# Twenty-four key/value units spread otherwise over an attention kernel: six, not eight, ahead of the first head pair

## The chip, the cores and the metric

One core of a Trainium2 chip (trn2) runs the whole kernel in one launch. The metric is the device time of one execution in microseconds, lower is better. Before: a median of 2206.81 us over 3 runs (2203.21 to 2211.9).

## What is computed

`x` is 8 images of 768 channels by 32x32 places (1024 tokens), float32. Layer 0 is group norm, a token attention with 12 heads of 64, and a residual; layer 1 is group norm, a per-channel integer shift with a separable 3x3 filter, and a residual. The attention is unusual: query and key enter only by their variance over the 64 channels of a head, so each head's scores are the outer product of two vectors.

```
qkv = tokens(gn(x)) @ W_qkv.T ;  q, k, v per head of 64
scores = var(v) x var(k) * 64**-0.5          # 1024 x 1024, rank one
x = x + proj(softmax(scores) @ v) + b_proj
x = x + depthwise3x3(shift(gn(x), offset))
```

## The kernel before, in words

**One image** goes through four stages. *Phase C* of the image before (line 1182): the projection, 12 tiles of 128x512 outputs, each 18 matmuls. *Phase A* (1152): the first key/value units. A unit (1076) is 36 fp16 matmuls that make k and v of two blocks of 128 tokens for one pair of heads; 4 units (`UQ`) make a pair and 24 an image. *The span* (1162): 6 pairs `p` of heads, each with 8 steps `m` of 128 keys. At each step ScalarE makes two tiles of exponentials (`exps`, 583), VectorE adds them up for the denominator (`add_up`, 786; steps 1 to 6 of pairs 0 to 3, 1 to 4 of pairs 4 and 5), and TensorE weighs v with them (`weigh`, 1117); a pair ends with the denominators on TensorE (1108, called at 1180). The units of pairs 2 to 5 are put into the steps of pairs 0 to 3, two at m = 0 and two at m = 4. `run` (276) makes image 0 by itself, loops six times over the middle images and ends with the last two; all but image 0 also do layer 1 of the image before inside the span.

**What a unit leads to.** VectorE takes its statistics (`kv_stats`, 742), ScalarE copies v out (`v_evict`, 576). Unit u + 2 waits for both, since they share two PSUM banks. After a pair's fourth unit VectorE forms the variances (`variances`, 752), TensorE transposes them (`k_transpose`, 1098), VectorE takes the key maximum and copies the row `at` (`k_max`, 767), TensorE spreads the maximum (`k_spread`, 1104), and VectorE makes the coefficients (`k_scales`, 777) with which that pair's exponentials start. SyncE writes `at` to HBM (`a_write`, 383) and reads it back broadcast to 128 partitions (`a_broadcast`, 387), the input of `exps`.

**What a pair's end leads to.** ScalarE copies the denominators (`d_copy`, 600, at m = 3 of the next pair), SyncE moves them in four small DMAs (`d_rows`, 396), VectorE inverts them (`d_reciprocal`, 802, at m = 2 in its own order), SyncE writes and broadcasts them (`r_write`, 402, `r_broadcast`, 406), VectorE normalises (`o_normalise`, 806), ScalarE and VectorE split the result in two fp16 parts (`o_first`, 611, `o_second`, 813). After pair 5 nothing of the span is left beside this, and the projection of the last part waits for it.

**What sets the order.** Each engine runs its own list in order, written out by hand in `span` and `phase_a` of each engine (SyncE 416, ScalarE 623, VectorE 862, TensorE 1152); semaphore waits stand in the list, so a wait holds up all behind it. VectorE's span before is

```
add_up(m) ; m=2: d_reciprocal, kv_stats ; m=3: kv_stats, k_max, taps_y, gn
m=4: k_scales, o_normalise ; m=5: kv_stats ; m=6: kv_stats, variances, taps_x ; m=7: o_second
```

The next image's `x` is loaded over `h_sp` (the input of all units) from ScalarE's queue, once no unit reads it any more; its statistics go over HBM on SyncE's queue (`stats_to_groups`, 324) in `group_end` (923). In image 0, `beside_a` (1204) transposes the 12 pieces of the projection's weights beside phase A.

Of the kernel before, what the change touches and what calls it, by code (L numbers as in the profile page):

```python
# [38 lines left out]
def gn_attention_displace(nc, x, w_qkv, w_proj, b_proj, offset, out):  # L39
# [17 lines left out]
    PC = 4 * HD  # L57
    UQ = MT // 2
    NU = NP * UQ
    RING = 8  # L60
# [22 lines left out]
    with ctx:  # L83
# [239 lines left out]

        def stats_to_groups(sp, k, b):
            sp.wait_ge(s_stat[k], b + 1)
            sp.dma_start(cs_rows[k].rearrange("(t p) s -> p t s", p=P), mv[k][:, :, :]).then_inc(s_cs[k], 16)
            sp.wait_ge(s_cs[k], b * 16 + 16)
            sp.dma_start(gin[k][:, :, :], cs_rows[k].rearrange("(g c) s -> g c s", c=GC)).then_inc(s_gin[k], 16)

        def stats_out(sp, k, b):  # L330
# [51 lines left out]
        def _(sp):  # L382
# [33 lines left out]
            def span(b, l1, with_next):  # L416
                later = l1 is not None
                a_write(b, 0)
                a_broadcast(b, 0, later)
                for p in range(NP):  # L420
                    if p == 0:
                        a_write(b, 1)
                        a_broadcast(b, 1, later)
                        continue
                    d_rows(b, p - 1)
                    r_write(b, p - 1)
                    if p < NP - 1:
                        a_write(b, p + 1)
                    r_broadcast(b, p - 1, later)
                    if p < NP - 1:  # L430
                        a_broadcast(b, p + 1, later)
                d_rows(b, NP - 1)
                r_write(b, NP - 1)
                r_broadcast(b, NP - 1, later)
                if with_next:
                    stats_to_groups(sp, "x", b + 1)
                    stats_out(sp, "x", b + 1)
                    stats_to_channels(sp, "x", b + 1)
# [116 lines left out]
        def _(act):  # L555
# [4 lines left out]
            def make_h(b):  # L560
# [4 lines left out]
                for t in range(CT + 1):  # L565
# [3 lines left out]
                    if t:  # L569
                        h_first(b, t - 1)  # L570

            def load_x(b, tiles):
                for t in tiles:
                    act.dma_start(x_in[:, t, :], x_t[b, :, t, :]).then_inc(s_xin[t], 16)
# [48 lines left out]
            def phase_a(b, beside=None):  # L623
                for u in range(2 * UQ - 1):
                    v_evict(b, u)
                    if beside is not None:
                        beside(u)

            def span(b, l1, with_next, beside=None):
                later = l1 is not None  # L630
                for p in range(NP):
                    nxt = (p + 2) * UQ
                    for m in range(MT):
                        if not later and p == 0 and m == 3:
                            act.wait_ge(s_pads, 2 * CT * 16)
                        exps(b, p, m)
                        if m == 1 and p == 0:
                            v_evict(b, 2 * UQ - 1)
                        if m == 3:
                            if p:  # L640
                                d_copy(b, p - 1, later)
                            if later:
                                middle_tap(l1, p)
                            if p <= 3:
                                v_evict(b, nxt)
                                v_evict(b, nxt + 1)
                        if m == 7:
                            if p:
                                o_first(b, p - 1)
                            if 1 <= p <= 4:  # L650
                                add_bias(b, p - 1)
                            if p <= 3:
                                v_evict(b, nxt + 2)
                                v_evict(b, nxt + 3)
                        if with_next and (p, m) in ((4, 1), (4, 4), (4, 7)):
                            load_x(b + 1, (2 * (m // 3), 2 * (m // 3) + 1))
                        if beside is not None:
                            beside(p, m)
# [12 lines left out]
            def beside_a(u):  # L671

                if u == 2:
                    act.wait_ge(s_scale, 2)
                if u >= 2:
                    weight_first(WKU + 2 * (u - 2))
                    weight_first(WKU + 2 * (u - 2) + 1)

            def beside_span(p, m):

                if (p, m) == (0, 0):
                    for w in range(2 * (2 * UQ - 1 - 2), WU - WKU):
                        weight_first(WKU + w)
                if (p, m) == (1, 0):
                    act.wait_ge(s_sub, 1)
                    nc.scalar.activation(taps[:, :, :, :], taps[:, :, :, :], ACT.Exp, scale=-2.0).then_inc(s_tapexp, 1)
# [34 lines left out]
        def _(dve):  # L721
# [140 lines left out]
            def phase_a(b, l1, beside=None):  # L862
                for u in range(2 * UQ - 1):
                    kv_stats(b, u)
# [17 lines left out]
            def span(b, l1, with_next, beside=None):  # L882
                later = l1 is not None
                for p in range(NP):
                    nxt = (p + 2) * UQ
                    if p == 0:
                        kv_stats(b, 2 * UQ - 1)
                        variances(b, 1)
                    for m in range(MT):
                        add_up(b, p, m, later)  # L890
                        if m == 2:
                            if p:
                                d_reciprocal(b, p - 1)
                            if p <= 3:
                                kv_stats(b, nxt)
                        if m == 3:
                            if p <= 3:
                                kv_stats(b, nxt + 1)
                            if p <= 4:
                                k_max(b, p + 1, later)  # L900
# [4 lines left out]
                        if m == 4:  # L905
                            if p <= 4:
                                k_scales(b, p + 1)
                            if p:
                                o_normalise(b, p - 1)
                        if m == 5 and p <= 3:  # L910
                            kv_stats(b, nxt + 2)
                        if m == 6:
                            if p <= 3:
                                kv_stats(b, nxt + 3)
                                variances(b, p + 2)
                            if later:
                                taps_x(l1, p, t_t)
                        if m == 7 and p:
                            o_second(b, p - 1)
                        if beside is not None:  # L920
                            beside(p, m)

            def group_end(b, with_next):
                if with_next:
                    x_stats(b + 1, range(4))
                d_reciprocal(b, NP - 1)
                if with_next:
                    x_stats(b + 1, (4, 5))
                    channel_aggregate("x", b + 1)
                o_normalise(b, NP - 1)  # L930
                o_second(b, NP - 1)
                if with_next:
                    group_var(dve, "x", b + 1)
                for u in range(PU):
                    t, j = divmod(u, 2)
                    dve.wait_ge(s_pj, b * PU + u + 1)
                    if j == 0:
# [3 lines left out]
                                                   ALU.mult, ALU.add).then_inc(s_x1, 1)  # L941
                    if with_next and u == 1:
                        group_spread_x(dve, b + 1, H_UP)
                    if with_next and u >= PU - CT:
# [8 lines left out]
            def first():  # L953
# [79 lines left out]
                def beside_a(u):  # L1033
# [4 lines left out]
                    if u >= 2:  # L1038
                        weight_second(WKU + 2 * (u - 2))
                        weight_second(WKU + 2 * (u - 2) + 1)  # L1040

                def beside_span(p, m):

                    if (p, m) == (0, 0):
                        for w in range(2 * (2 * UQ - 1 - 2), WU - WKU):
                            weight_second(WKU + w)
                    for at_, stage in (((0, 3), displacements), ((0, 7), window_starts), ((1, 3), normalise_taps), ((1, 7), masks)):
# [27 lines left out]
        def _(pe):  # L1075
# [76 lines left out]
            def phase_a(b, later, beside=None):  # L1152
                for u in range(2 * UQ):
                    kv_unit(b, u, later)
# [7 lines left out]
            def span(b, later):  # L1162
                for p in range(NP):
                    nxt = (p + 2) * UQ
                    for m in range(MT):
                        if m in (0, 4) and p <= 3:
                            kv_unit(b, nxt + m // 2, later)
                            kv_unit(b, nxt + m // 2 + 1, later)
                        if m == 0 and p <= 4:
                            k_transpose(b, p + 1)  # L1170
                        weigh(b, p, m, later)
                        if m == 2 and p <= 4:
                            k_spread(b, p + 1)
# [30 lines left out]
            def beside_a(u):  # L1204

                if u >= 2:
                    for w in (2 * (u - 2), 2 * (u - 2) + 1):
                        if w == 0:
# [45 lines left out]
```

## Time and profile before

| | |
|---|---|
| median of 3 runs | 2206.81 us (2203.21 to 2211.9) |
| the profiled execution | 2203.28 us, of which the span is 2201.7 |
| TensorE busy (matmuls) | 2016.2 us, 92% |
| VectorE busy | 1674.7 us, 76% |
| ScalarE busy | 1172.8 us, 53% |
| mean granted TensorE clock | 0.965 |

Of the profile three things are read: who ends last (the chain of waits that ends with the last instruction), the timeline of each engine through one image, and the granted clock of TensorE in short stretches. Times below are us from the span's start. Images are counted 0 to 7 and pairs 0 to 5, as in the code; image 2 runs from about 578 to 838 and is the one shown.

### The profile page before, as it was taken

The numbers are of one execution on the slowest core, as the hardware profiler recorded it, in microseconds if no ns is written. First come the engines' busy times: TensorE is split into PE (matmuls) and PEld (weight loads), VectorE is DVE, ScalarE is ACT, GpSimd is POOL, SyncE is SP. The second block draws the span as 40 slices with busy tenths as digits, with TensorE's granted clock in tenths as the row PEclk, the third lists the DMA queues.
The fourth block names the chain that finished last, engine by engine and source line by source line (L and its number), as shares of the span: only waits on it lengthen the run. The fifth ranks groups of instructions, "written<-read, shape, count | busy, mean of one in ns | idle before, by whom it ended". The sixth has DMA issues, their size and how long they took to land.

```text
span 2201.7 us, 36306 instructions
## 1 busy us (share of the span) xinstructions
PE 2016.2 (92%) x13036; PEld 1114.0 (51%) x13036; DVE 1674.7 (76%) x3695; ACT 1172.8 (53%) x1285; POOL 157.6 (7%) x215
## 2 busy tenths in 40 slices
PE   3999899989999899998999979998999989999970
PEld 2765257643666337562475525754366533765230
DVE  7677567887688875987778976788668887688738
ACT  5466625664266743667336752566427674266701
POOL 2000000010000000100000100000000110011101
PEclk8999999999999999999999989999999999999995
DMA  6412302344033511335122440234313351133304
GB/s 231 157 43 59 97 11 88 117 135 126 13 103 109 186 57 40 106 120 169 31 69 98 144 146 12 97 107 147 115 33 102 99 183 49 42 115 116 115 20 172
DMA packets 106985, 219.10 MB, mean 100 GB/s; under 512 B 53025, under 2 KB 53793, under 8 KB 106785
## 3 DMA queue, kind: packets, MB, share of 16 engines
q1 hardware_dynamic: 74816, 100.12, 15.6%
q0 software_dynamic: 25920, 94.38, 12.0%
q10 hardware_dynamic: 6048, 22.02, 2.8%
q8 instruction: 114, 1.87, 0.4%
q14 instruction: 87, 0.70, 0.1%
HBM read 158.28 MB, written 57.80 MB: 98 GB/s over the span
## 4 chain that ended last, share of the span: by engine, by line
PE 74%; DVE 9%; DMA 7%; ACT 4%; issue 3%; SPq 2%; POOL 1%; ACTq 0%; DVEq 0%; POOLq 0%
PE ps L1092 29%; PE ps L1131 25%; PE ps L1146 14%; PE ps L1113 4%; ACT ring L597 3%; DMA dt_sb<-d_sb 3%; DVE bt L800 2%; SPq L400 1%; DVE st L749 1%; DMA bt<-r_rows 1%; DMA cs_rows_y<-mv_y 1%; PE ps L1106 1%; DMA xv<-in_L_conv_W_qkv 1%; POOL ring L530 1%; DVE h_sp L740 0%
## 5 line engine op out<-in xcount | busy, mean ns | idle before, releaser
L597 ACT ACTIVATE ring<-a_sb,coef 128x1024 f32<-128x1024 f32 x768 | 809.9, 1137 | 53.9 <-PE ps L1131 53.3
L1092 PE MATMUL ps<-wkv_hi,h_sp 128*128 128x256 f16 x4608 | 776.3, 274 | 13.3 <-DVE h_sp L740 11.2
L1131 PE MATMUL ps<-ring,xv 128*64 128x512 f32 x3072 | 709.1, 608 | 0.0
L1092 PE MATMUL ps<-wkv_lo,h_sp 128*128 128x256 f16 x2304 | 630.1, 273 | 0.0
L1092 PEld LDWEIGHTS ps<-wkv_hi,h_sp 128*128 128x128 f16 x4608 | 451.9, 98 | 119.1 <-issue 50.0
L800 DVE TENSOR_TENSOR bt<-bt,ring 128x1024 f32<-128x1024 f32 x416 | 488.5, 1215 | 2.1 <-ACT ring L597 2.1
L1131 PEld LDWEIGHTS ps<-ring,xv 128*64 128x64 f32 x3072 | 209.7, 139 | 408.5 <-issue 388.7
L581 ACT ACTIVATE xv<-ps 128x256 f32<-128x256 f32 x192 | 73.4, 382 | 612.1 <-DVE st L749 612.1
L1146 PE MATMUL ps<-xv,wp_hi 128*128 128x512 f16 x1152 | 351.1, 383 | 18.3 <-issue 11.9
L749 DVE BATCH_NORM_STATS2 st<-ps 128x6 f32<-128x64 f32 x1536 | 217.8, 213 | 98.7 <-PE ps L1092 97.8
L1092 PEld LDWEIGHTS ps<-wkv_lo,h_sp 128*128 128x128 f16 x2304 | 225.9, 98 | 26.4
L1146 PE MATMUL ps<-xv,wp_lo 128*128 128x512 f16 x576 | 220.4, 383 | 0.0
L1146 PEld LDWEIGHTS ps<-xv,wp_hi 128*128 128x128 f16 x1152 | 113.5, 98 | 176.2 <-issue 37.0
L800 DVE TENSOR_TENSOR bt<-ring 128x1024 f32<-128x1024 f32 x96 | 115.4, 1221 | 46.2 <-PE ps L1113 33.4
L804 DVE RECIPROCAL dt_sb<-dt_sb 128x16 f32<-128x16 f32 x48 | 12.1, 253 | 172.5 <-DMA dt_sb<-d_sb 172.5
L614 ACT ACTIVATE xv<-bt 128x1024 f16<-128x1024 f32 x48 | 50.4, 1050 | 140.4 <-DVE bt L811 140.4
L940 DVE SCALAR_TENSOR_TENSOR xv<-ps,proj_f,xv 128x512 f32<-128x512 f32 x96 | 70.2, 738 | 53.4 <-PE ps L1146 52.9
L811 DVE TENSOR_TENSOR bt<-ps,bt 128x1024 f32<-128x1024 f32 x48 | 58.5, 1220 | 46.2 <-DMA bt<-r_rows 46.2
L1146 PEld LDWEIGHTS ps<-xv,wp_lo 128*128 128x128 f16 x576 | 56.8, 99 | 65.5 <-issue 1.6
L1113 PE MATMUL ps<-ring,ones 128*32 128x512 f32 x640 | 85.2, 605 | 0.0
L567 ACT ACTIVATE ring<-h_sp,rb_x 128x1024 f32<-128x1024 f32 x42 | 51.0, 1229 | 51.2 <-DMA rb_x<-gs_rows_x 51.2
L490 POOL DMA_INDIRECT bt<-shift_rows,first_i x42 | 54.5, 1298 | 257.3 <-DMA shift_rows<-bt 224.7
(122 smaller groups left out, 1305.2 us busy)
## 6 DMA issues: line engine op xcount, KB each, us to landing
a_sb<-a_rows SPq DMA_DIRECT2D x96, 512.0 KB, 6.1
xv<-in_x POOLq DMA_DIRECT2D x48, 512.0 KB, 3.6
bt<-r_rows SPq DMA_DIRECT2D x96, 256.0 KB, 4.0
h_sp<-in_x ACTq DMA_DIRECT2D x42, 512.0 KB, 4.4
shift_rows<-bt POOLq DMA_DIRECT2D x42, 512.0 KB, 6.4
out<-xv POOLq DMA_DIRECT2D x42, 512.0 KB, 3.5
shift_rows<-ring SPq DMA_DIRECT2D x12, 528.0 KB, 14.9
xv<-in_L_conv_W_qkv SPq DMA_DIRECT2D x4, 1152.0 KB, 9.1
```

Source lines behind the costliest of these rows:

```text
L490: nc.gpsimd.indirect_dma_start(dst, None, shift_rows[t].rearrange("c r -> (c r)").unsqueeze(0), bass.IndirectOffsetOnAxis(first_i[:, t:t + ...
L567: nc.scalar.activation(y_t[t], x_in[:, t, :], ACT.Identity, bias=rb["x"][:, t, 1:2], scale=rb["x"][:, t, 0:1]).then_inc(s_hf, 1)
L581: nc.scalar.activation(v_sb[:, q, 2 * g:2 * g + 2, :], src[:, :, 0:P], ACT.Copy, scale=V_DOWN).then_inc(s_vev, 1)
L597: nc.scalar.activation(ring_of(p, s, m), a_sb[:, h % 4, :], ACT.Exp, scale=coef[:, h, m:m + 1]).then_inc(s_exp, 1)
L749: ins = nc.vector.bn_stats(st[:, 2 * g + m, c, :], ps[:, kv_bank[u % 2], lo:lo + HD])
L800: nc.vector.tensor_tensor(acc_of(p, s), one, ring_of(p, s, m), ALU.add).then_inc(s_acc, 1)
L811: nc.vector.tensor_tensor(r2, ps[:, k:k + 2, :], r2, ALU.mult).then_inc(s_on, 1)
L940: nc.vector.scalar_tensor_tensor(cut, ps[:, pj_bank[u % 6], :], proj_f[:, 0:1], cut, ALU.mult, ALU.add).then_inc(s_x1, 1)
L1092: last = nc.tensor.matmul(ps[:, kv_bank[u % 2], half * 2 * P:(half + 1) * 2 * P], h_sp[:, k, hp, m * P:(m + 1) * P], wkv[wpart][:, k, q * ...
L1113: last = nc.tensor.matmul(ps[32 * g:32 * g + 32, D_BANK, :], ones[:, 0:32], tiles[s][:, j * HALF:(j + 1) * HALF], start=start, stop=stop)
L1131: last = nc.tensor.matmul(ps[s * HD:(s + 1) * HD, o_bank[p % 2] + j, :], v_sb[:, p, m, s * HD:(s + 1) * HD], ring_of(p, s, m)[:, j * HALF: ...
L1146: last = nc.tensor.matmul(ps[:, pj_bank[u % 6], :], wp[wpart][:, k, t * P:(t + 1) * P], o_sp[:, k, op, j * HALF:(j + 1) * HALF], start=(k ...
```

## The change

Units 0 to 5 instead of 0 to 7 stand in phase A (`UA`), and all later ones move two places: pairs 0 to 3 make four each and pair 4 makes the last two. So a pair's last two units are now made in the pair before it, at m = 0. What follows from a unit moves with it on each engine: `variances(p + 1)` from m = 6 of the pair before to m = 3, `k_max` to m = 4 and `k_scales` to m = 6 for p up to 3, `k_transpose` behind `weigh(p, 3)`. `d_copy` is at m = 2 in pair 5. The loads of x come later and one or two at a time; the statistics of x are spread differently; SyncE writes them ahead of `r_broadcast` of pair 5 and does `r_broadcast` ahead of `a_write`. In image 0 three pieces of weights, not two, are transposed after a unit. The number of instructions of each kind is the same.

```diff
+    UA = UQ + 2
 (SyncE; stats_to_groups is cut in stats_write and stats_read)
                     d_rows(b, p - 1)
                     r_write(b, p - 1)
+                    r_broadcast(b, p - 1, later)
                     if p < NP - 1:
                         a_write(b, p + 1)
-                    r_broadcast(b, p - 1, later)
-                    if p < NP - 1:
                         a_broadcast(b, p + 1, later)
                 d_rows(b, NP - 1)
                 r_write(b, NP - 1)
+                if with_next:
+                    stats_write(sp, "x", b + 1)
                 r_broadcast(b, NP - 1, later)
                 if with_next:
-                    stats_to_groups(sp, "x", b + 1)
+                    stats_read(sp, "x", b + 1)
...
 (ScalarE)
+            X_LOADS = {(4, 3): (0, 1), (5, 0): (2,), (5, 1): (3,), (5, 4): (4,), (5, 5): (5,)}
...
-                for u in range(2 * UQ - 1):
+                for u in range(UA):
                     v_evict(b, u)
...
-                    nxt = (p + 2) * UQ
+                    nxt = UA + p * UQ
...
                         exps(b, p, m)
-                        if m == 1 and p == 0:
-                            v_evict(b, 2 * UQ - 1)
+                        if p and m == (3 if p <= 4 else 2):
+                            d_copy(b, p - 1, later)
                         if m == 3:
-                            if p:
-                                d_copy(b, p - 1, later)
                             if later:
                                 middle_tap(l1, p)
-                            if p <= 3:
+                            if p <= 4:
                                 v_evict(b, nxt)
                                 v_evict(b, nxt + 1)
...
-                        if with_next and (p, m) in ((4, 1), (4, 4), (4, 7)):
-                            load_x(b + 1, (2 * (m // 3), 2 * (m // 3) + 1))
+                        if with_next and (p, m) in X_LOADS:
+                            load_x(b + 1, X_LOADS[p, m])
...
 (VectorE; phase_a as on ScalarE)
-                    nxt = (p + 2) * UQ
-                    if p == 0:
-                        kv_stats(b, 2 * UQ - 1)
-                        variances(b, 1)
+                    nxt = UA + p * UQ
                     for m in range(MT):
                         add_up(b, p, m, later)
                         if m == 2:
                             if p:
                                 d_reciprocal(b, p - 1)
-                            if p <= 3:
+                            if p <= 4:
                                 kv_stats(b, nxt)
                         if m == 3:
-                            if p <= 3:
+                            if p <= 4:
                                 kv_stats(b, nxt + 1)
-                            if p <= 4:
+                                variances(b, p + 1)
+                            if p == 4:
                                 k_max(b, p + 1, later)
...
                         if m == 4:
-                            if p <= 4:
+                            if p <= 3:
+                                k_max(b, p + 1, later)
+                            if p == 4:
                                 k_scales(b, p + 1)
                             if p:
                                 o_normalise(b, p - 1)
...
                             if p <= 3:
                                 kv_stats(b, nxt + 3)
-                                variances(b, p + 2)
+                                k_scales(b, p + 1)
...
                         if m == 7 and p:
+                            if p == NP - 1 and with_next:
+                                x_stats(b + 1, (0, 1))
                             o_second(b, p - 1)
...
             def group_end(b, with_next):
                 if with_next:
-                    x_stats(b + 1, range(4))
+                    x_stats(b + 1, (2, 3))
                 d_reciprocal(b, NP - 1)
                 if with_next:
                     x_stats(b + 1, (4, 5))
                     channel_aggregate("x", b + 1)
                 o_normalise(b, NP - 1)
+                if with_next:
+                    group_var(dve, "x", b + 1)
                 o_second(b, NP - 1)
                 if with_next:
-                    group_var(dve, "x", b + 1)
+                    group_spread_x(dve, b + 1, H_UP)
...
-                    if with_next and u == 1:
-                        group_spread_x(dve, b + 1, H_UP)
...
-                        weight_second(WKU + 2 * (u - 2))
-                        weight_second(WKU + 2 * (u - 2) + 1)
+                        for w in range(3 * (u - 2), 3 * (u - 1)):
+                            weight_second(WKU + w)
...
 (TensorE)
-                for u in range(2 * UQ):
+                for u in range(UA):
                     kv_unit(b, u, later)
...
-                        if m in (0, 4) and p <= 3:
+                        if m == 0 and p <= 4 or m == 4 and p <= 3:
                             kv_unit(b, nxt + m // 2, later)
                             kv_unit(b, nxt + m // 2 + 1, later)
-                        if m == 0 and p <= 4:
+                        if m == 4 and p <= 3:
+                            k_spread(b, p + 1)
+                        weigh(b, p, m, later)
+                        if p <= 4 and m == (3 if p <= 3 else 1):
                             k_transpose(b, p + 1)
-                        weigh(b, p, m, later)
-                        if m == 2 and p <= 4:
+                        if m == 3 and p == 4:
                             k_spread(b, p + 1)
```

## Rows read from the trace of the kernel before

**Rows 1.** The page: span, busy times, the last-ending chain by engine.

```profile
span 2201.7 us, 36306 instructions
PE 2016.2 (92%) x13036; PEld 1114.0 (51%) x13036; DVE 1674.7 (76%) x3695; ACT 1172.8 (53%) x1285; POOL 157.6 (7%) x215
PE 74%; DVE 9%; DMA 7%; ACT 4%; issue 3%; SPq 2%; POOL 1%; ACTq 0%; DVEq 0%; POOLq 0%
```

**Rows 2.** The chain in image 2, pairs 2 to 4 (start, us, what).

```profile
676.58 7.97 PE ps L1092 x72
...
684.76 5.30 PE ps L1131 x24
...
767.80 1.85 PE ps L1113 x16
```

**Rows 3.** TensorE's timeline: the wait in pair 4, images 2 and 7.

```profile
754.03 0.58 PE L1106 MATMUL ps<-kdiag,ones 2*128 2x2 f32 x2 [6.84 <-DVE kdiag L775]
...
2052.35 0.38 PE L1106 MATMUL ps<-kdiag,ones 2*128 2x2 f32 x2 [4.97 <-DVE kdiag L775]
```

**Rows 4.** Busy time by stretch: the granted clock is the number ahead of the DMA pair.

```profile
747.20:754.00 6.80, 0.00 (x0) 0.00 (x0) 3.10 (x7) 4.60 (x5) 0.00 (x0) 0.86 0.37 134
754.00:756.00 2.00, 1.97 (x6) 1.03 (x8) 1.96 (x2) 0.00 (x0) 0.00 (x0) 0.50 0.15 57
```

**Rows 5.** ScalarE's timeline in image 2, pairs 0 to 4.

```profile
609.25 4.36 ACT L597 ACTIVATE ring<-a_sb,coef 128x1024 f32<-128x1024 f32 x4
...
637.20 8.43 ACT L597 ACTIVATE ring<-a_sb,coef 128x1024 f32<-128x1024 f32 x8 [0.34 <-PE ps L1131]
...
669.70 8.43 ACT L597 ACTIVATE ring<-a_sb,coef 128x1024 f32<-128x1024 f32 x8
678.03 0.58 ACT L604 ACTIVATE d_sb<-ps 128x512 f32<-128x512 f32 x1
...
703.54 8.41 ACT L597 ACTIVATE ring<-a_sb,coef 128x1024 f32<-128x1024 f32 x8
711.85 0.58 ACT L604 ACTIVATE d_sb<-ps 128x512 f32<-128x512 f32 x1
...
735.64 1.14 ACT L597 ACTIVATE ring<-a_sb,coef 128x1024 f32<-128x1024 f32 x1
```

**Rows 6.** VectorE's timeline in image 2, pairs 2 to 4.

```profile
683.99 0.25 DVE L804 RECIPROCAL dt_sb<-dt_sb 128x16 f32<-128x16 f32 x1 [3.76 <-DMA dt_sb<-d_sb]
...
687.42 1.14 DVE L749 BATCH_NORM_STATS2 st<-ps 128x6 f32<-128x64 f32 x8
...
703.26 0.22 DVE L756 TENSOR_TENSOR dm<-st 128x32 f32<-128x32 f32 x1
...
704.22 1.27 DVE L854 SCALAR_TENSOR_TENSOR xv<-bt,taps,xv 128x1024 f32<-128x1024 f32 x1
...
716.09 0.25 DVE L804 RECIPROCAL dt_sb<-dt_sb 128x16 f32<-128x16 f32 x1 [2.35 <-DMA dt_sb<-d_sb]
...
750.90 0.25 DVE L804 RECIPROCAL dt_sb<-dt_sb 128x16 f32<-128x16 f32 x1 [5.07 <-DMA dt_sb<-d_sb]
```

**Rows 7.** The page's groups: `o_normalise`.

```profile
L811 DVE TENSOR_TENSOR bt<-ps,bt 128x1024 f32<-128x1024 f32 x48 | 58.5, 1220 | 46.2 <-DMA bt<-r_rows 46.2
```

**Rows 8.** SyncE's queue behind pair 5 of image 2.

```profile
800.18 0.33 SPq L404 DMA_DIRECT2D r_rows<-dt_sb  x1
801.65 1.12 SPq L413 DMA_DIRECT2D bt<-r_rows  x2
803.21 0.38 SPq L326 DMA_DIRECT2D cs_rows_x<-mv_x  x1
```

**Rows 9.** TensorE waiting behind pair 5, and image 0's phase A on VectorE.

```profile
811.35 27.38 PE ps L1146 x126
...
70.35 1.15 DVE L749 BATCH_NORM_STATS2 st<-ps 128x6 f32<-128x64 f32 x8 [2.39 <-PE ps L1092]
72.42 1.14 DVE L968 SCALAR_TENSOR_TENSOR wp_lo<-ps,scale,wp_hi 128x384 f16<-128x384 f32 x2 [0.92 <-ACT wp_hi L669]
```

More of the change, by code:

```diff
@@ L322, in gn_attention_displace, with stats_write, stats_read, stats_to_groups @@
         GV = {"x": 3, "y": 1}
-        def stats_to_groups(sp, k, b):
+        def stats_write(sp, k, b):
             sp.wait_ge(s_stat[k], b + 1)
             sp.dma_start(cs_rows[k].rearrange("(t p) s -> p t s", p=P), mv[k][:, :, :]).then_inc(s_cs[k], 16)
+        def stats_read(sp, k, b):
             sp.wait_ge(s_cs[k], b * 16 + 16)
             sp.dma_start(gin[k][:, :, :], cs_rows[k].rearrange("(g c) s -> g c s", c=GC)).then_inc(s_gin[k], 16)
+        def stats_to_groups(sp, k, b):
+            stats_write(sp, k, b)
+            stats_read(sp, k, b)
         def stats_out(sp, k, b):
@@ L675, in beside_a @@
                 if u >= 2:
-                    weight_first(WKU + 2 * (u - 2))
-                    weight_first(WKU + 2 * (u - 2) + 1)
+                    for w in range(3 * (u - 2), 3 * (u - 1)):
+                        weight_first(WKU + w)
             def beside_span(p, m):
-                if (p, m) == (0, 0):
-                    for w in range(2 * (2 * UQ - 1 - 2), WU - WKU):
-                        weight_first(WKU + w)
                 if (p, m) == (1, 0):
@@ L862, in phase_a @@
             def phase_a(b, l1, beside=None):
-                for u in range(2 * UQ - 1):
+                for u in range(UA):
                     kv_stats(b, u)
@@ L1038, in beside_a @@
                     if u >= 2:
-                        weight_second(WKU + 2 * (u - 2))
-                        weight_second(WKU + 2 * (u - 2) + 1)
+                        for w in range(3 * (u - 2), 3 * (u - 1)):
+                            weight_second(WKU + w)
                 def beside_span(p, m):
-                    if (p, m) == (0, 0):
-                        for w in range(2 * (2 * UQ - 1 - 2), WU - WKU):
-                            weight_second(WKU + w)
                     for at_, stage in (((0, 3), displacements), ((0, 7), window_starts), ((1, 3), normalise_taps), ((1, 7), masks)):
@@ L1152, in phase_a @@
             def phase_a(b, later, beside=None):
-                for u in range(2 * UQ):
+                for u in range(UA):
                     kv_unit(b, u, later)
@@ L1163, in span @@
                 for p in range(NP):
-                    nxt = (p + 2) * UQ
+                    nxt = UA + p * UQ
                     for m in range(MT):
-                        if m in (0, 4) and p <= 3:
+                        if m == 0 and p <= 4 or m == 4 and p <= 3:
                             kv_unit(b, nxt + m // 2, later)
                             kv_unit(b, nxt + m // 2 + 1, later)
-                        if m == 0 and p <= 4:
+                        if m == 4 and p <= 3:
+                            k_spread(b, p + 1)
+                        weigh(b, p, m, later)
+                        if p <= 4 and m == (3 if p <= 3 else 1):
                             k_transpose(b, p + 1)
-                        weigh(b, p, m, later)
-                        if m == 2 and p <= 4:
+                        if m == 3 and p == 4:
                             k_spread(b, p + 1)
@@ L1206, in beside_a @@
                 if u >= 2:
-                    for w in (2 * (u - 2), 2 * (u - 2) + 1):
+                    for w in range(3 * (u - 2), 3 * (u - 1)):
                         if w == 0:
```

## The prediction

> **What bounds the kernel now.** The page comes first: TensorE is busy 92% of the span and holds 74% of the chain that ends last [rows 1]. Then the chain through image 2. In pairs 0 to 3 nothing but TensorE stands in it: 72 matmuls for two units in 7.97 us, 24 for three steps of weighing in 5.30 [rows 2], so a pair is 2 x 7.97 for four units, 8 x 1.77 for eight steps, 0.5 for the key maximum and 1.85 for denominators, 32.5 us. In pair 4 there are no units and TensorE stands: `k_spread` waits 6.84 us for VectorE's `kdiag`, 4.97 in image 7 [rows 3]. The granted clock falls behind it, to 0.50, which is the level of 1.2 GHz [rows 4]; the 24 matmuls after it need 7.47 instead of 5.30, 2.2 us more. So pair 4 has 9.0 us an image to give, and two units are 7.97.
>
> Next VectorE and ScalarE, which aren't behind by much. Write E(p) for the first exponentials of pair p: 609.25 for pair 0, then 637.20, 669.70, 703.54, 735.64 [rows 5]. The last three steps are 32.5, 33.8 and 32.1, a mean of 32.8. That is a loop of its own, as long as TensorE's 32.5: E(p), 8.33 us of ScalarE up to `d_copy`; the four small DMAs up to the reciprocal, 5.96 and 4.24 (678.03 to 683.99, 711.85 to 716.09 [rows 5, 6]); then VectorE's list, 19.55 up to the next E(p) (683.99 to 703.54). Before the change this loop costs nothing, since `k_max` for pair p + 1 rests on variances made a pair's half earlier, and ScalarE is 15 us ahead of the weighing.
>
> **The change, part by part.** TensorE does the same matmuls, so the gain is at most its idle time. The question is when pair p + 1's key maximum is ready, which the change ties to the reciprocal.
>
> *The late statistics.* `variances(p + 1)` now stands behind `d_reciprocal`, unit statistics, one add of two tiles, and statistics again. From the reciprocal to the second statistics is 3.43 (683.99 to 687.42), the statistics hold VectorE 1.06, and the variances 1.07 (0.12 of waiting and 703.26 to 704.22) [rows 6]: ready 5.55 after the reciprocal. I call this moment T. TensorE stands at `k_transpose` from the end of step 3 until T, with the next two units and all later steps queued behind it.
>
> *The loop.* The variances enter it (+1.07); `k_scales` stays in it, at its end, where it replaces a copy-out (-0.2). So reciprocal to E(p + 1) is 20.4, not 19.55: +0.85 a pair, and the mean loop becomes 33.7, more than TensorE's 32.5.
>
> *Pair 0.* E(0) is taken as before: `a_broadcast` sets it, and its inputs (units 0 to 3) don't move. From 609.25 the second tile of step 1 is there at 613.55; its add 1.15, step 2's 2.26, statistics 1.06, step 3's 2.26, statistics and variances 2.13: T is 622.4. TensorE, with 7.97 less ahead of it, would be there at 619.6; it waits 3. Then 20.4 - 5.55 - 1.1 (no `o_normalise` in pair 0 [rows 7]) gives E(1) = 636.2, about 0.8 earlier than 637.20.
>
> *Pairs 1 to 3.* E(4) = 735.64 - 0.8 + 3 x 0.85, and 0.2 for `a_broadcast`, which is written after the later `k_max` and now lands about when E is due: 737.6. Pair 3 ends on TensorE about 740 (its T, then transposes 0.2, two units 7.97, `k_spread` 0.3, four steps 7.1 and denominators 1.85: 17.45), only 1.4 earlier than before, though two units less are done.
>
> *Pair 4.* TensorE makes the two units and steps 0 and 1 (7.97 + 3.5) and stands from about 751.7. E(4) + 8.33 + DMAs + 5.55 is the last T. The DMAs took 6.95 here before (743.95 to 750.90 [rows 6]), beside x's loads; those now come later, so I take 5.2, near the mean of 5.96 and 4.24. T = 756.7: a wait of 5.0 takes the place of 6.84. Behind T: transposes 0.2, six steps 10.6 with 0.3 of switching, `k_spread` 0.3, three denominators beside steps and the last, 3.9: 15.3. The clock: after 4.97 or 6.84 of standing it fell, so it falls after 5.0; I take 1.7, a little under the 2.2. Pair 4 ends at 773.7, not 767.80 + 1.85 = 769.65 [rows 2]: **+4.0 an image**, six times. In image 7 the wait before was 1.9 shorter and the low clock about 0.5 cheaper: +6.4. Pair 5 is all TensorE, 23.6, and moves as a whole.
>
> *Behind pair 5.* The reciprocal is at 799.9, `r_write` at 800.18, `r_broadcast` at 801.65; the statistics of x are written at 803.21, as soon as VectorE has aggregated them [rows 8]. With `stats_write` ahead, `r_broadcast` is issued at 803.21 + 0.38 + 0.05, **2.0 later**, and normalising, `o_first`, `o_second` and TensorE's last part of the projection, for which it stands until 811.35 [rows 9], all hang on it. Seven images load a next x: +14. What the earlier `group_var` and `group_spread_x` give is nothing: from 811.35 on the chain is 27.38 of pure matmul [rows 9].
>
> *Image 0.* After each of four units a third weight transpose needs the bank of the first. Unit 2's statistics start at 70.35 and that bank is read out at 72.42 + 0.6, while TensorE would be there at 70.9: 2.1 each [rows 9]. 8.6 of new waits against 7.97 of units moved, and 0.9 of waiting at T: about +1.5, and pair 4 has no x loads or layer 1 in its way and is filled. I take +2.
>
> *The other edits* (`d_copy` at m = 2 in pair 5, x loads one by one, `r_broadcast` ahead of `a_write`) cost nothing: each of them lies beside TensorE's 23.6 in pair 5 or makes earlier what was not waited for. If that cover goes, `o_second` of pair 4 and the statistics are late, a few us an image at most.
>
> **Sum.** 6 x 4.0 + 6.4 + 14 + 2 = 46. The profiled execution is 2203.3, 3.5 under the median of 2206.8; 2206.8 + 46 = **2253**, 2.1% slower. A measurement of this kernel can tell about 0.5%, 11 us.
>
> **Rivals.**
> *A: the gap is filled (faster).* Mechanism: pair 4 has idle TensorE, pairs 0 to 3 none, and units moved there cost nothing. It decides if T comes before TensorE gets to it. Each of seven images gains 9.0 and loses 2.0 behind pair 5: 2207 - 49 = 2158. For it: the 6.84 and the half clock. Against it: T rests on the reciprocal, and there VectorE is already 3 to 5 us late for the new order. Chance 0.08. The Trainium skill (Perfetto Trace Analysis, Optimization Strategy) says that where the most-contended engine changes over time, interleaving the regimes may help; pairs 0 to 3 and pair 4 are such regimes here, and by this rule alone the time would be that of this rival.
> *B: the small DMAs get shorter*, 4.2 as the best row has it, in every pair. The loop is then 20.4 + 8.33 + 4.2 = 33.0, E(4) 735.3, T 753.4, pair 4 ends at 770.4: +0.8. 6 x 0.8 + 3 + 14 + 2 = 24: 2231, still slower. Chance 0.14. If besides the write behind pair 5 costs nothing: +10, 2217, the edge of no change. Chance 0.06.
> *C: the broadcasts are late.* `a_broadcast` lands 1 us after E is due in pairs 1 to 3 (+3 an image) or `r_broadcast` shares the DMA engines with the 6 KB of tiny pieces ahead of it: 7 x 3 more, 2275. Chance 0.12. By the Trainium skill (DMA: Bandwidth & Descriptors, Queues, rings and completion order) descriptors of one ring are consumed in order, so the statistics' go first; it gives no price that the trace shows, and no run here has that order.
> My own case has 0.60.
>
> **Range and chances.** The own case is 2253, down 14 if the clock stays up and the loop grows less, up 12 with part of C. The range takes B and C in: 2225 to 2277; A and B's edge are left out. Faster 0.08, within 0.5% 0.06, slower 0.86.
>
> **What the profile would show.** TensorE's matmuls of `k_transpose` waiting for VectorE in every pair of images 1 to 7: 3 us in pair 0, 0 to 2 in pairs 1 to 3, 5 in pair 4, and no wait at `k_spread`. E(p) in steps of 33.7. The half clock still in pair 4. `r_broadcast` 3.8 us after the reciprocal behind pair 5, not 1.75. Period of an image about 266 instead of 260. I am wrong if TensorE doesn't wait at `k_transpose`, if E(p) goes on in steps of 32.5 or less, or if the last part of the projection starts no later after pair 5.

## The result, and the profile after

The changed kernel takes 2266.05 us, median of 4 runs (2257.91 to 2267.5), against 2207.5 of the kernel before on the same chip. The ratio is **1.0259**, 95% interval 1.0238 to 1.028: slower by 58.6 us. The profiled execution took 2257.9, 54.6 more than the one shown of before. The forecast was 2253 and slower; the time lies in its range of 2225 to 2277.

The page after the change, span, busy times and the chain by engine (for [rows 1]):

```profile
span 2256.3 us, 36312 instructions
PE 2036.6 (90%) x13036; PEld 1118.5 (50%) x13036; DVE 1676.5 (74%) x3695; ACT 1179.1 (52%) x1285; POOL 192.3 (9%) x215
PE 37%; DVE 27%; DMA 13%; ACT 10%; issue 8%; SPq 3%; POOL 1%; DVEq 0%; ACTq 0%; POOLq 0%
```

The work is the same, the chain is not. TensorE held 74% of it and holds 37%; VectorE, DMA and ScalarE took the rest. No engine has become busier to speak of: what grew is waiting from one to the next.

The most telling reading is a table of stages. A stage ends where the denominators of a pair end on TensorE, where `o_second` of pair 5 ends, and where the projection's last tile is taken up by VectorE. Each number is after minus before, in us, worked out from the two timelines (image 0's first stage starts with the span, that of the others where the projection of the image before ends):

| image | phase A, pair 0 | pairs 1 to 3 | pair 4 | pair 5 | up to `o_second` | projection |
|---|---|---|---|---|---|---|
| 0 | +1.7 | -0.5 | +0.2 | 0 | +3.4 | +2.1 |
| 1 | -3.6 | +1.4 | +5.3 | 0 | +4.1 | +1.9 |
| 2 | -4.0 | +0.7 | +4.8 | 0 | +3.0 | +1.7 |
| 7 | -4.1 | +2.0 | +6.9 | 0 | -0.2 | 0 |
| all eight | **-21.0** | **+7.0** | **+35.6** | 0 | **+24.9** | **+8.3** |

So 21.6 us were lost in the spans and 33.2 behind pair 5. Now the lines. TensorE's timeline in image 2, the waits for the key maximum in pair 0 and pair 4 (for [rows 3]):

```profile
638.71 0.28 PE L1105 MATMUL ps<-ident,av 128*16 128x128 f32 x1 [2.98 <-DVE kmx L770]
...
770.02 0.28 PE L1105 MATMUL ps<-ident,av 128*16 128x128 f32 x1 [4.15 <-DVE kmx L770]
```

The wait at `k_spread` is gone, and one at `k_transpose` stands in its place, 4.15 us instead of 6.84, with one of 2.98 in pair 0 that was not there before. VectorE's timeline, pair 4 of image 2, shows why (for [rows 6]):

```profile
764.33 0.25 DVE L809 RECIPROCAL dt_sb<-dt_sb 128x16 f32<-128x16 f32 x1 [3.39 <-DMA dt_sb<-d_sb]
764.50 1.08 DVE L754 BATCH_NORM_STATS2 st<-ps 128x6 f32<-128x64 f32 x8
765.50 2.34 DVE L805 TENSOR_TENSOR bt<-bt,ring 128x1024 f32<-128x1024 f32 x2
767.76 1.14 DVE L754 BATCH_NORM_STATS2 st<-ps 128x6 f32<-128x64 f32 x8
768.93 0.21 DVE L761 TENSOR_TENSOR dm<-st 128x32 f32<-128x32 f32 x1
...
769.80 0.16 DVE L770 TENSOR_REDUCE kmx<-m 128x2 f32<-128x16 f32 x1
```

From the reciprocal at 764.33 to the maximum at 769.96 is 5.6 us, and ahead of the reciprocal VectorE stands 3.39 for four small DMAs. ScalarE's timeline of image 2 gives the loop (for [rows 5]):

```profile
652.38 8.43 ACT L607 ACTIVATE ring<-a_sb,coef 128x1024 f32<-128x1024 f32 x8
...
685.64 8.43 ACT L607 ACTIVATE ring<-a_sb,coef 128x1024 f32<-128x1024 f32 x8 [0.18 <-issue]
...
718.65 8.43 ACT L607 ACTIVATE ring<-a_sb,coef 128x1024 f32<-128x1024 f32 x8
...
751.77 8.43 ACT L607 ACTIVATE ring<-a_sb,coef 128x1024 f32<-128x1024 f32 x8 [0.18 <-issue]
```

Steps of 33.3, 33.0 and 33.1, over TensorE's 32.5; the first of them is longer in most other images, up to 35.7. Granted clock around the wait in pair 4, by stretch (for [rows 4]), the number ahead of the DMA pair:

```profile
762.00:769.00 7.00, 3.87 (x19) 1.06 (x17) 4.63 (x20) 0.45 (x2) 0.00 (x0) 1.00 0.34 97
...
771.00:773.00 2.00, 2.00 (x8) 0.63 (x6) 1.97 (x4) 2.00 (x3) 0.00 (x0) 0.50 1.00 397
```

The clock falls to half here too, as behind the longer wait before. SyncE's queue behind pair 5 of image 2 (for [rows 8]), and TensorE's chain after it (for [rows 9]):

```profile
817.25 0.33 SPq L411 DMA_DIRECT2D r_rows<-dt_sb  x1
820.28 0.38 SPq L327 DMA_DIRECT2D cs_rows_x<-mv_x  x1
820.78 1.12 SPq L420 DMA_DIRECT2D bt<-r_rows  x2
825.29 0.34 SPq L331 DMA_DIRECT2D gin_x<-cs_rows_x  x1
```

```profile
813.66 3.29 DMA dt_sb<-d_sb
...
821.32 6.71 DMA bt<-r_rows
...
831.81 29.07 PE ps L1150 x126
```

`r_broadcast` is issued 3.81 after the reciprocal of 816.97 instead of 1.75. It also takes longer: its two halves land 6.2 and 7.2 us after the first issue, before 3.5 and 6.0. And the projection's 126 matmuls take 29.07, not 27.38: the granted clock is 0.52 from 831.8 to 835.0 (mean 0.94 over 831.8 to 860.9, before 1.00).

### The profile page after: what moved, and what is told of

Read it like the earlier page. It is cut to its first block, busy times and chain, and to the rows that moved or that the text cites. A ratio compares the mean times of both kernels' runs of the same rounds, so it can differ in the third digit from the quotient of the medians.

```text
span 2256.3 us, 36312 instructions
## 1 busy us (share of the span) xinstructions
PE 2036.6 (90%) x13036; PEld 1118.5 (50%) x13036; DVE 1676.5 (74%) x3695; ACT 1179.1 (52%) x1285; POOL 192.3 (9%) x215
## 4 chain that ended last, share of the span: by engine, by line
PE 37%; DVE 27%; DMA 13%; ACT 10%; issue 8%; SPq 3%; POOL 1%; DVEq 0%; ACTq 0%; POOLq 0%
PE ps L1150 13%; PE ps L1135 12%; DVE bt L805 10%; PE ps L1096 9%; ACT ring L607 8%; DVE st L754 6%; DMA a_sb<-a_rows 3%; DMA dt_sb<-d_sb 3%; PE ps L1117 3%; SPq L407 3%; DMA bt<-r_rows 2%; DMA a_rows<-at 2%; DVE bt L849 2%; DVE bt L846 1%; DVE bst_x L728 1%
## 5 line engine op out<-in xcount | busy, mean ns | idle before, releaser
L607 ACT ACTIVATE ring<-a_sb,coef 128x1024 f32<-128x1024 f32 x768 | 810.7, 1136 | 48.5 <-DMA a_sb<-a_rows 33.1
L1096 PE MATMUL ps<-wkv_hi,h_sp 128*128 128x256 f16 x4608 | 786.8, 276 | 11.8 <-DVE h_sp L745 9.9
L1150 PE MATMUL ps<-xv,wp_hi 128*128 128x512 f16 x1152 | 358.9, 389 | 41.0 <-DVE xv L820 28.3
L498 POOL DMA_INDIRECT bt<-shift_rows,first_i x42 | 83.4, 1986 | 162.8 <-DMA shift_rows<-bt 117.1
L506 POOL DMA_DIRECT2D shift_rows<-bt x42 | 23.3, 556 | 633.1 <-DVE bt L834 633.1
```

The lines of the kernel that those rows point to most:

```text
L498: nc.gpsimd.indirect_dma_start(dst, None, shift_rows[t].rearrange("c r -> (c r)").unsqueeze(0), bass.IndirectOffsetOnAxis(first_i[:, t:t + ...
L607: nc.scalar.activation(ring_of(p, s, m), a_sb[:, h % 4, :], ACT.Exp, scale=coef[:, h, m:m + 1]).then_inc(s_exp, 1)
L1096: last = nc.tensor.matmul(ps[:, kv_bank[u % 2], half * 2 * P:(half + 1) * 2 * P], h_sp[:, k, hp, m * P:(m + 1) * P], wkv[wpart][:, k, q * ...
L1150: last = nc.tensor.matmul(ps[:, pj_bank[u % 6], :], wp[wpart][:, k, t * P:(t + 1) * P], o_sp[:, k, op, j * HALF:(j + 1) * HALF], start=(k ...
```

## The experiments

Ratios are each against the kernel before on the chip of the run (2214.4, 2214.8 or 2211.4 us there), so they are compared, not the microseconds. Line numbers shift by a few between kernels.

### e1_bcast_first

```diff
                 r_write(b, NP - 1)
-                if with_next:
-                    stats_write(sp, "x", b + 1)
                 r_broadcast(b, NP - 1, later)
                 if with_next:
+                    stats_write(sp, "x", b + 1)
                     stats_read(sp, "x", b + 1)
```

> The changed kernel with r_broadcast of pair 5 ahead of stats_write again; VectorE's order stays (group_var ahead of o_second). Theory: SyncE's order costs about 3 us an image behind pair 5, but group_var now waits for statistics that come over HBM as late as before, with o_second queued behind it, so only part comes back: the end of pair 5's denominators to the end of o_second goes from 21 us to 19 to 20, the time from about 2265 to 2250. Rival (the order on SyncE is all of it): 18 us, as before, and about 2232. Rival (SyncE's order costs nothing, the transfer is only slow there): 21 us and no change.

2241.39 us, ratio 1.0122 (1.0098 to 1.0146). Up to `o_second` 17.8 to 20.4 us in images 1 to 6 (before 16.2 to 18.3), +11.9 in all. VectorE's timeline behind pair 5 of image 2:

```profile
818.93 1.22 DVE L815 TENSOR_TENSOR bt<-ps,bt 128x1024 f32<-128x1024 f32 x1 [4.77 <-DMA bt<-r_rows]
821.41 0.17 DVE L356 TENSOR_REDUCE gs_x<-gin_x 32x1 f32<-32x24 f32 x1 [1.25 <-DMA gin_x<-cs_rows_x]
...
822.75 1.23 DVE L819 TENSOR_TENSOR xv<-bt,xv 128x1024 f16<-128x1024 f32 x1
```

The broadcast is early again, but `group_var` waits 1.25 us for the statistics with `o_second` queued behind it. Half of the change's loss goes with one line on SyncE. The expectation of about 2250 was too high, the one for the stage right.

### e2_old_tail

As e1, and on VectorE:

```diff
-                if with_next:
-                    group_var(dve, "x", b + 1)
                 o_second(b, NP - 1)
                 if with_next:
+                    group_var(dve, "x", b + 1)
                     group_spread_x(dve, b + 1, H_UP)
```

> The changed kernel with r_broadcast first and group_var behind o_second, so that only group_spread_x and the x statistics are placed otherwise than before the change. Theory: the 33 us lost behind pair 5 come back but for some clock: 18 us from the denominators to o_second, about 2232. Rival (the spread ahead of the projection's evictions or the later loads of x are the cause): over 2250.

2234.27 us, ratio 1.0099 (1.0071 to 1.0126). Against the kernel before, the stage up to `o_second` is +2.3 us in all and the projection +3.5; of the change's 33 us 27 are gone. The spread and x's loads are cleared of it. What is left, 1%, belongs to the spans.

### e10_group_var_behind

The fourth corner: the same edit on VectorE, SyncE's order as in the change.

> The changed kernel with group_var and its spread behind o_second of pair 5, stats_write staying ahead of r_broadcast: the fourth corner beside the changed kernel, e1 and e2. Theory: with the broadcast late, the statistics are there when VectorE comes to group_var, so its place costs only its own 0.35 us beyond o_first: 21 us from the denominators to o_second stay 20.5 to 21, ratio 1.023 to 1.026. Rival (VectorE's order costs the same in both orders of SyncE, about 2 us an image as e1 against e2 has it): ratio about 1.02.

2264.5 us, ratio 1.0243 (1.0224 to 1.0261); the stage up to `o_second` is +26.3 in all, the change's is +24.9. The interval overlaps that of the change. So `group_var`'s place costs nothing that can be told while the broadcast is late. When it is not, the stage shows a cost (+11.9 in all in e1, +2.3 in e2, 1.1 to 2.2 us an image between normalising and `o_second`), though the intervals of the two times overlap.

### e3_before_stats_first

The kernel before with the opposite of e1:

```diff
                 r_write(b, NP - 1)
+                if with_next:
+                    stats_write(sp, "x", b + 1)
                 r_broadcast(b, NP - 1, later)
                 if with_next:
-                    stats_to_groups(sp, "x", b + 1)
+                    stats_read(sp, "x", b + 1)
```

> The kernel before with one edit: stats_write ahead of r_broadcast of pair 5. Theory: r_broadcast is issued 2.0 us later and lands about 1 us slower still, seven times, and the clock falls in the longer wait: 3 to 5 us an image, 2207 + 20 to 35 = about 2235. Rival (only the issue is later, nothing is shared on the DMA engines): +14, 2221. Rival (the tail's cost belongs to VectorE's order): no change.

2245.73 us, ratio 1.0148 (1.0122 to 1.0175): 31 us, in the upper part of the 20 to 35 expected. Up to `o_second` +25.1, projection +8.0: the same two numbers as in the change (+24.9 and +8.3), in a kernel that has nothing else of it. In all seven images the first half of the broadcast lands 6.3 to 6.7 us after its issue; in e1 and e2 it is 3.4 to 3.7. This is the cleanest result of the study.

### e4_late_transpose

Pair 4 in the order of pairs 0 to 3:

```diff
-                        if p <= 4 and m == (3 if p <= 3 else 1):
+                        if p <= 4 and m == 3:
                             k_transpose(b, p + 1)
-                        if m == 3 and p == 4:
+                        if m == 5 and p == 4:
                             k_spread(b, p + 1)
 (VectorE: k_max at m = 4 and k_scales at m = 6 for p = 4 too)
```

> The changed kernel with pair 4 ordered as pairs 0 to 3: k_transpose of pair 5 behind step 3 and not step 1, k_spread behind step 5, k_max at m = 4 and k_scales at m = 6 on VectorE. Nothing is taken out. Theory: the 4.15 us of waiting at k_transpose in pair 4 shrink to under 1, the clock stays up there, but pair 5's exponentials start later: pair 4 goes from 32.8 to 28 to 29 us, the time down by 25 to 35, to about 2235. Rival (the bound in pair 4 is VectorE's list and not the place of the transpose): pair 4 or 5 get longer by what is taken away, and the time stays within 10 of 2265.

2258.49 us, ratio 1.0198 (1.0152 to 1.0245). Pair 4 went from +35.6 to +21.2, pair 5 from 0 to +7.5. TensorE's waits in pair 4 of one image:

```profile
770.15 0.28 PE L1102 MATMUL ps<-ident,av 128*16 128x128 f32 x1 [0.72 <-DVE kmx L770]
772.68 5.26 PE L1132 MATMUL ps<-ring,xv 128*64 128x512 f32 x16 [2.14 <-ACT ring L607]
```

The wait at the transpose shrank to 0.72 as the theory said, but right behind the transposes TensorE now waits 2.14 for exponentials, and pair 5 is longer. The 25 to 35 us didn't come: the intervals of e4 and of the change overlap a little (up to 1.0245, from 1.0238), and by stages e4's profiled run is +56.0 against +54.9. That e4 is faster at all is not shown; the rival, within 10 us, holds. So the place of the transpose alone was not the bound. That the lateness of VectorE's list was, e5 has to show.

### e5_stats_ahead

The changed kernel, on VectorE:

```diff
                         if m == 2:
-                            if p:
-                                d_reciprocal(b, p - 1)
                             if p <= 4:
                                 kv_stats(b, nxt)
+                                kv_stats(b, nxt + 1)
+                                variances(b, p + 1)
+                            if p:
+                                d_reciprocal(b, p - 1)
                         if m == 3:
-                            if p <= 4:
-                                kv_stats(b, nxt + 1)
-                                variances(b, p + 1)
```

> The changed kernel with one move on VectorE: the statistics of both units made at m = 0 and the variances stand ahead of d_reciprocal (all at m = 2), so they no longer wait for the four small DMAs. Nothing is taken out. Theory (the key maximum is tied to the reciprocal): the waits at k_transpose go, 3.0 to about 1 us in pair 0, 4.15 to 0 in pair 4 with the clock staying up, pair 4 goes from 32.8 to about 27, the loop of exponentials falls under TensorE's 32.5: 8 to 10 us an image, ratio to the kernel before about 1.00 (0.99 to 1.00). Rival (VectorE is simply full, so the order of its list matters little): pair 4 stays over 31 and the ratio over 1.015.

2197.8 us, ratio **0.9926** (0.9908 to 0.9943): 3.2% off the changed kernel by the order of one list, and faster than before although the slow tail is still in it (+24.8 and +10.1). VectorE in pair 4 of image 2:

```profile
748.89 1.15 DVE L754 BATCH_NORM_STATS2 st<-ps 128x6 f32<-128x64 f32 x8 [2.58 <-PE ps L1095]
...
750.94 0.16 DVE L770 TENSOR_REDUCE kmx<-m 128x2 f32<-128x16 f32 x1
751.02 0.24 DVE L809 RECIPROCAL dt_sb<-dt_sb 128x16 f32<-128x16 f32 x1
```

The maximum starts 0.9 us behind the end of the second unit's statistics, with only the variances between, and the reciprocal has no wait left: VectorE waits 2.58 us for TensorE's unit where it waited for the DMAs, and these land meanwhile. All waits of TensorE for the maximum in this kernel:

```profile
PEld ps L1104 <- DVE kmx L770: 10.3, 7, 1.6
PE ps L1104 <- DVE kmx L770: 4.2, 6, 0.7
```

In the changed kernel they are 90.2 and 58.7. Pair 4 is 26.92 in every image, pairs 1 to 3 are 97.02, both TensorE's own time.

### e6_dcopy_early

```diff
-                        if p and m == (3 if p <= 4 else 2):
+                        if p and m == 2:
                             d_copy(b, p - 1, later)
```

> The changed kernel with d_copy at m = 2 in every pair, two exponentials earlier, so that the reciprocal and all behind it come 2.1 us earlier. Theory: the wait in pair 4 falls from 4.15 to about 2, with less clock lost, and pairs 1 to 3 to TensorE's 32.5: 3 to 4 us an image, ratio about 1.013. Rival (the wait is set by something else on VectorE): no change, 1.026.

2243.84 us, ratio 1.0122 (1.0098 to 1.0146), as expected. In images 1 to 7 pairs 1 to 3 fell to 97.0 to 97.4, pair 4 to 30.3 to 33.1. Less came back in pair 4 than 2.1 us of earlier `d_copy` promise, and its wait at `k_transpose` fell to 2.3 to 3.5, not to about 2: up to pair 4 the small DMAs now take 5.5 to 6.1 us where they took 4.2. What they share the engines with at that time was not singled out.

### e7_late_loads

The kernel before with the loads of x placed as in the change (`X_LOADS`) and nothing else.

> The kernel before with only the loads of x placed as in the change, later and one by one. Theory: the four small DMAs in pair 4 take 5 to 5.5 us instead of 6.9, so k_spread's wait there falls from about 7 to 5.5: 1.5 to 2 us an image in six images, ratio 0.993 to 0.996. Rival (the loads are not what lengthens them): no change; or slower, if the loads now land beside pair 5's small DMAs and those behind it.

2197.64 us, ratio **0.9927** (0.9906 to 0.9947). Pair 4 is 14.6 us shorter in all. `d_copy` to reciprocal there took 6.3 to 7.4 us in images 0 to 6 and takes 4.3 to 5.2; the waits at `k_spread`:

```profile
PEld ps L1108 <- DVE kdiag L777: 52.5, 13, 6.4
PE ps L1108 <- DVE kdiag L777: 41.3, 10, 5.5
```

The longest on the second of these lines was 8.6 before. The small DMAs of pair 5 got longer in images 1 to 6 (6.5 to 8.9 us, before 5.2 to 5.5), and pair 5 stayed at 23.6. One part of the change is a gain by itself. It is in e1, e2, e5 and e8 too, and what it is worth there was not measured.

### e8_ahead_old_tail

e5 and e2 together.

> The changed kernel with the move of e5 and the tail of e2 (r_broadcast first, group_var behind o_second). Theory: both costs are gone and their sum holds: e5's gain of 8 to 10 us an image and e2's 3 to 4, so it is faster than the kernel before, ratio 0.980 to 0.988. Rival (the gain in pair 4 is given back in pair 5 or behind it): 0.995 or more.

2165.88 us, ratio **0.9783** (0.9766 to 0.98). By stages against before: -38.1, -4.2, -6.9, +7.5, +3.4, +0.4. A part of the gain is given back in pair 5, about 1 us an image, where TensorE waits for exponentials; that is far less than the rival asked for. Against e2, which differs by the order of VectorE's list alone, it is 3.1% faster. TensorE is back to 72% of the chain:

```profile
PE 72%; DVE 11%; DMA 10%; issue 4%; ACT 2%; SPq 1%; POOL 1%; ACTq 0%; DVEq 0%; POOLq 0%
```

### e9_three_banks

e8, and for the weights of image 0:

```diff
-            bank = ps[:, 4 + u % 2, 0:3 * P].rearrange("p (q c) -> p q c", c=P)
+            bank = ps[:, 4 + (u - WKU) % 3, 0:3 * P].rearrange("p (q c) -> p q c", c=P)
...
-                        if w >= 2:
-                            pe.wait_ge(s_wlo, WKU + w - 1)
+                        if w >= 3:
+                            pe.wait_ge(s_wlo, WKU + w - 2)
```

> The kernel of e8 with three PSUM banks, not two, for the transposed weights of the projection in image 0, so that the third transpose after a unit waits for nothing that is still being read. Theory: the four waits of 2.1 us in phase A of image 0 go, 6 to 8 us once (0.3%), ratio 0.975 against e8's 0.978. Rival (pair 0's exponentials or VectorE are late there anyway): under 2 us.

2155.29 us, ratio **0.9749** (0.973 to 0.9768), the fastest kernel here: 2.5% under the kernel before, 5% under the changed one. In the changed kernel TensorE's timeline of image 0 has, after unit 2,

```profile
71.62 0.55 PE L1207 MATMUL ps<-ident,bt 128*128 128x128 f32 x3 [2.20 <-DVE wp_lo L975]
```

and three more such waits of 2.12 to 2.18. In e9 the stage of phase A and pair 0 in image 0 is 8.3 us shorter than in e8 (120.6 against 128.9).

## Why the prediction was right, and where it was not

**The bound and the mechanism.** As written: the key maximum is tied to the reciprocal (5.6 us against 5.55), TensorE stands at `k_transpose` with all behind it. The waits were 2.98 in pair 0 (forecast 3), 4.15 in pair 4 (5.0), and the clock fell behind the latter. e5 is the proof: it takes out nothing, only puts the statistics ahead of the wait, and 3.2% of the time goes. Rival A said that units moved into pair 4 cost nothing; in the change this was wrong, and in e5 and e8 it is what happens, once T comes early enough. The rival's condition was the right one, its size (9.0 us an image) too high: the spans of images 1 to 7 are 44 us shorter in e8, not 63.

**The spans, forecast +30.4 for images 1 to 7 and +2 for image 0; measured +20.3 and +1.4.** The term that was mis-sized is the small DMAs. I took 5.2 us before the reciprocal, from rows of before; in the changed kernel they take 4.2 in pairs 2 to 4 in nearly every case, which is rival B's price, and 4.4 to 5.5 in pair 1. So the loop is 33.0 to 33.2 in images 1 to 6, not 33.7. The wait in pair 4 hardly shrank with it, since TensorE gets there earlier too: in image 2 pair 3 ended 3.3 us earlier than before, and not 1.4. Against the shorter DMAs stands a piece of rival C that I had set at 0.2: in pair 1 of five images the second head's `a_broadcast` is late. ScalarE's timeline in image 1:

```profile
381.79 1.15 ACT L607 ACTIVATE ring<-a_sb,coef 128x1024 f32<-128x1024 f32 x1 [0.28 <-PE ps L1135]
384.42 7.38 ACT L607 ACTIVATE ring<-a_sb,coef 128x1024 f32<-128x1024 f32 x7 [1.48 <-DMA a_sb<-a_rows]
```

The two together give the number: E(1) to E(2) took 33.3 to 35.7 in images 1 to 7, in all 13.3 over seven times 33.0, and with rival B's 7.8 (6 x 0.8 + 3) that is 21.1, near the 20.3 measured. Why this broadcast is late in five images and not in two, no run here tells.

**Behind pair 5, forecast +14; measured +33.2.** The later issue was right to the tenth (3.81 against 3.8): over images 0 to 6 it is 14.0 us. The step that failed is the price of the order on the queue: the sum had only the issue, 7 x 2.0, and put the landing at nothing. The broadcast's second half, which `o_normalise` needs, lands 0.9 to 1.7 us later after its issue, 9.1 in all (the first half 2.7 in image 2); `group_var` ahead of `o_second` adds 0.13 an image, 0.43 in one; the reciprocal comes 0.9 later in all. These make up the stage. The longer wait then costs 1.6 to 2.1 us of half clock in five of the seven projections; all of them together come to +8.3. Rival C held the sharing at +3 an image with a chance of 0.12; e3 shows 2.7 over the later issue, with nothing else changed.

The rule of the Trainium skill (DMA: Bandwidth & Descriptors, Queues, rings and completion order), that descriptors of a ring are taken in order, agrees with the trace: in image 2 the 768 pieces of the statistics start 0.4 to 0.9 us after the broadcast's issue, its own first packet 2.0 us after it. The price isn't told by that order alone. Before, the first packet started 1.3 us after the issue, and none of the 128 packets of 4 KB took over 0.32 us; now 24 of them take over 0.5, up to 2.3 (in images 0 to 6 it is 9 to 24 packets over 0.5 us, before 0 to 5). Two microseconds from the first packet on, before and after, with the same share of the DMA engines' time (0.84, 0.81) and a fifth of the rate (244, 47 GB/s):

```profile
802.90:804.90 2.00, 2.00 (x11) 0.90 (x10) 0.28 (x4) 0.00 (x0) 0.00 (x0) 1.00 0.84 244
...
822.70:824.70 2.00, 2.00 (x11) 0.89 (x10) 0.00 (x0) 0.00 (x0) 0.00 (x0) 1.00 0.81 47
```

No other queue moves a packet between this issue and this landing, in image 2 before or after, so the load of other queues is not the cause. Why a packet behind the pieces is slow, no run here tells.

**Image 0.** +1.7 up to the end of pair 0 against +1.5; the four waits of 2.1 us were there, and e9 takes them out.

**The total** was right to 13 us because one term was 10 too high and another 19 too low. That both errors lay opposite ways is luck. So the sum hides how far both parts were off: the one by half of what was measured, the other by more than half.

**The other rule** of the Trainium skill (Perfetto Trace Analysis, Optimization Strategy), that interleaving regimes of different bounds may help, gave rival A, and the change's own time spoke against it. e8 is -38 us in the profiled runs with that interleaving, the later loads among it. In this kernel it pays under a condition: what makes the moved work ready must not hang on another engine's last wait.

## What to carry to other kernels

Work moved into an engine's idle stretch brings its consumers along; before counting the idle time, find in each consumer's list the wait that it now stands behind, and put what needs no such wait ahead of it. In a queue shared by a critical and an uncritical transfer, the critical one goes first, even if the other is tiny. Test each edit of a bundle by itself: here one edit (later loads) was worth -0.7%, one cost +1.5%, and the main one, with those loads, came to +1% (e2) or -2% (e8) by the order of four calls.

## What was not expected of the hardware

A write of 6 KB in 8-byte pieces issued 0.5 us ahead of a 512 KB broadcast on the same queue lengthened the broadcast's first half from 3.5 to 6.2 us and its second from 6.0 to 7.2; the same write issued 1.6 us behind it leaves the first half alone. It isn't free there either: behind pair 5 of image 7, where there are no statistics to write, the second half lands after 4.7 us, in images 0 to 6 of the kernel before after 5.7 to 6.4. What it would give to keep the write away altogether was not tested. And the small DMAs of `d_rows` (2 KB each) took 4.2 us beside little traffic and up to 7.4 beside loads of 512 KB; issuing those loads one by one and later, with not a byte less, was worth 0.7% of the kernel before (in image 2 the second group of them is issued at 754.1 instead of 744.1, where the `d_copy` in pair 4 had just been done).
